# The last key tile's exponentials added by GpSimd into the last pair's sum, in a fused cross-attention and FFN kernel

## The reference, cut to what matters

```
scores = jnp.clip(jnp.einsum('bhsd,bhtd->bhst', q, k) / scale, -50.0, 50.0)
scores = jnp.where(attend, scores, -10000.0)
scores = jnp.clip(scores, -50.0, 50.0)
probs  = jax.nn.softmax(scores, axis=-1)
ctx    = jnp.einsum('bhst,bhtd->bhsd', probs, v)
```

## Time and profile before

| | |
|---|---|
| median of 3 runs | 1443.54 us (1441.85 to 1997.49) |
| the profiled execution | 1444.08 us |
| its span, first to last instruction | 1442.3 us |
| granted TensorE clock, mean | 0.998 of full speed |
| attention stage of the third entry | about 578 to 706 us in the span |
| its groups of 13 tiles | 30.95 and 30.63 us |

### The profile page before, as it was taken

How to read it: one execution, slowest core, us unless ns; L and a number is a source line. 1 busy time by engine, 2 the same in 40 slices (tenths; PEclk the granted TensorE clock), 3 DMA queues, 4 the chain that set the end, 5 groups by cost and what they waited for, 6 DMA issues and landing times. The chain is left out here.

```text
span 1442.3 us, 25135 instructions
## 1 busy us (share of the span) xinstructions
PE 1414.6 (98%) x10354; PEld 956.7 (66%) x10354; DVE 1108.7 (77%) x1659; ACT 813.2 (56%) x1021; POOL 90.1 (6%) x129
## 2 busy tenths in 40 slices
PE   9999999999999999999999999998999999999999
PEld 7886333787333688333689333486788888888887
DVE  7684999885999895899885799887865566655655
ACT  4345999435999535899635799634442333323331
POOL 1010000100000100000100000110010010100100
PEclk9999999999999999999999999999999999999999
DMA  8553000636000425000424600262345454354544
GB/s 264 143 209 152 9 10 10 190 95 240 28 10 10 147 97 189 27 17 10 141 74 173 247 12 14 59 264 103 146 147 189 167 206 167 146 190 176 207 158 175
DMA packets 54994, 180.91 MB, mean 125 GB/s; under 512 B 11249, under 2 KB 25841, under 8 KB 42721
## 3 DMA queue, kind: packets, MB, share of 16 engines
q1 hardware_dynamic: 39760, 116.08, 22.3%
q0 software_dynamic: 15120, 63.23, 12.9%
HBM read 111.97 MB, written 67.31 MB: 124 GB/s over the span
## 5 line engine op out<-in xcount | busy, mean ns | idle before, releaser
L1007 ACT ACTIVATE cx_probs<-cx_sc,proj_mbias 128x1024 f32<-128x1024 f32 (+1 forms) x416 | 442.8, 1113 | 49.9 <-PE cx_sc L1287 28.6
L1153 DVE TENSOR_SCALAR cx_probs<-cx_probs 128x1024 f32<-128x1024 f32 (+1 forms) x416 | 269.6, 683 | 52.1 <-ACT cx_probs L1007 50.1
L1119 DVE TENSOR_TENSOR cx_padd<-cx_probs,cx_probs 128x1024 f32<-128x1024 f32 x192 | 233.6, 1217 | 0.9
L1287 PEld LDWEIGHTS cx_sc<-cx_q,cx_kt 32*128 32x128 f32 (+1 forms) x2496 | 104.4, 180 | 192.8 <-ACT cx_probs L1007 173.0
L1310 PE MATMUL cx_acc<-cx_probs,cx_vt 128*32 128x512 f32 (+1 forms) x1664 | 219.0, 598 | 3.7 <-DVE cx_probs L1153 3.7
L1287 PE MATMUL cx_sc<-cx_q,cx_kt 32*128 32x512 f32 (+1 forms) x2496 | 207.7, 426 | 10.1 <-ACT cx_probs L1007 6.9
L140 PE MATMUL ff_yp<-hand_wds,ff_held 128*128 128x512 f32 x624 | 143.7, 389 | 0.1
L140 PEld LDWEIGHTS ff_yp<-hand_wds,ff_held 128*128 128x128 f32 x624 | 117.1, 188 | 24.8 <-DVE ff_kept L1832 0.5
L1769 DVE TENSOR_TENSOR ff_x<-ff_yp,ff_x 128x512 f32<-128x512 f32 x120 | 80.4, 688 | 58.4 <-PE ff_yp L140 57.7
L1322 PE MATMUL cx_tot<-cx_padd,cx_ones 128*32 128x256 f32 x1536 | 120.8, 390 | 0.0
L951 ACT ACTIVATE cx_kt<-cx_sc,proj_bk 128x256 fp32r<-128x256 f32 (+1 forms) x96 | 44.1, 478 | 70.2 <-PE cx_sc L140 69.8
(11 more groups left out here) (298 smaller groups left out, 2077.0 us busy)
## 6 DMA issues: line engine op xcount, KB each, us to landing
ff_x<-scr_x SPq DMA_DIRECT2D x30, 1024.0 KB, 5.0
scr_x<-ff_x SPq DMA_DIRECT2D x28, 1024.0 KB, 4.8
proj_raw<-in_ctxT SPq DMA_DIRECT2D x20, 512.0 KB, 6.0
hand_wds<-scr_wd POOLq DMA_DIRECT2D x7, 1024.0 KB, 10.0
scr_q<-cx_q SPq DMA_DIRECT2D x3, 2048.0 KB, 6.3
cx_wo<-scr_wo POOLq DMA_DIRECT2D x3, 2048.0 KB, 13.4
scr_xs<-cx_xs POOLq DMA_DIRECT2D x3, 2048.0 KB, 7.9
cx_q<-scr_q SPq DMA_DIRECT2D x3, 1536.0 KB, 10.5
```

The source lines that it names most:

```text
L1007: nc.scalar.activation(prob(N)[0:r], bank_of(n)[0:r], ACT.Exp, bias=mbias[0:r, b, t:t + 1], scale=SCALE).then_inc(exp_done, 1)
L1119: nc.vector.tensor_tensor(padd[z][(g * QP + j) % 2][:], prob(2 * i + z)[:], prob(2 * i + 2 + z)[:], ALU.add).then_inc(added[z], 1)
L1153: nc.vector.tensor_scalar(prob(N)[0:r], prob(N)[0:r], LOW, HIGH, ALU.max, ALU.min).then_inc(clip_done, 1)
L1287: last = nc.tensor.matmul(bank_of(2 * i + h // 2)[0:r, h % 2], kt[own, z, c, t * P:t * P + r], q[own, y, c], start=n == 0, stop=n == 2)
```

## The change

In the groups c = 0, 1 and 2 of each batch entry, `single` is no longer called. GpSimd gets a new function `last_tile`, which for z = 0 and 1 adds the 65 rows of the 13th tile's exponentials into rows 0 to 64 of the last pair sum (j = 5), in place. It waits for VectorE's add of that pair sum (`added`) and for the tile's clip (`clip_done`), and counts in a new semaphore `lent`. TensorE's `sums` of the last pair wait for both `lent`, and ScalarE's exponential that takes the 13th tile's buffer waits for `lent` in place of `single`. Group c = 3 stays as it was. The counts of `sums_done` are worked out anew, since a group now has 12 passes and only the fourth has 13. GpSimd's queue gets its six adds of an entry ahead of that entry's `beside(b)`, and those of the last entry at the end.

```
-    SUMS = 2 * QP + 1
+    PASSES = 2 * QP
...
+        def passes(g):
+            return g * PASSES + g // HC
         def sums_until(g, j):
-            return g * SUMS + 2 * j + 2 + (1 if j >= QP - 2 else 0)
+            return passes(g) + 2 * j + 2 + (1 if j >= QP - 2 and g % HC == HC - 1 else 0)
+        def lent_before(g):
+            return g - g // HC
...
+                def last_tile(b, c, z):
+                    g = b * HC + c
+                    N = (b * STEPS + (c + 1) * TT - 1) * 2 + z
+                    own = padd[z][(g * QP + QP - 1) % 2][0:TLAST]
+                    pool.wait_ge(added[z], (g + 1) * QP)
+                    pool.wait_ge(clip_done, N + 1)
+                    nc.gpsimd.tensor_tensor(own, own, prob(N)[0:TLAST], ALU.add).then_inc(lent[z], 1)
...
-                    pool.wait_ge(sums_done, (b + 1) * HC * SUMS)
+                    pool.wait_ge(sums_done, passes((b + 1) * HC))
...
-                for b in range(B - 1):
-                    beside(b)
+                for b in range(B):
+                    for c in range(HC - 1):
+                        for z in range(2):
+                            last_tile(b, c, z)
+                    if b < B - 1:
+                        beside(b)
...
-                    act.wait_ge(sums_done, (g + 1) * SUMS)
+                    act.wait_ge(sums_done, passes(g + 1))
...
+                        elif og % HC < HC - 1:
+                            act.wait_ge(lent[n % 2], lent_before(og) + 1)
                         else:
-                            act.wait_ge(sums_done, og * SUMS + SINGLE)
+                            act.wait_ge(sums_done, passes(og) + SINGLE)
...
                     for z in range(2):
+                        if j == QP - 1 and c < HC - 1:
+                            pe.wait_ge(lent[z], lent_before(g) + 1)
                         pe.wait_ge(added[z], g * QP + j + 1)
...
-                    if t == TT - 1:
+                    if t == TT - 1 and c == HC - 1:
                         single(b, c)
```

More of the change, by code:

```diff
@@ L790, in context @@
             "scores_done", "exp_done", "clip_done", "values_done", "sums_done"))
-        added = m.sems("added", 2)
+        added, lent = m.sems("added", 2), m.sems("lent", 2)
         acc_out, tot_out = m.sem("acc_out"), m.sem("tot_out")
```

## The result

The changed kernel takes 1485.89 us in the median of four runs (1484.71 to 1488.72), the kernel before 1441.85, 1443.54 and 1447.09 us beside it, with a fourth, far slower run of 1997.49 us that is left out: a ratio of 1.0285, 95% interval 1.0269 to 1.0301, so 2.7 to 3.0% slower. The profiled execution has a span of 1482.8 us where before had 1442.3, 40.5 more.

A forecast was written before the change was run, and what follows sets the result against it. TensorE, VectorE and ScalarE lay within a few per cent in attention, VectorE having 1.2 to 1.5 us free. Held, a group costs 34.05 us: 9.94 an entry, 39.8 in all, 1444.08 to 1483.9, less 0.5: 1483 us; range 1437 to 1496.

The forecast's parts named there:

- What decides is VectorE, held for the whole of each GpSimd add: Attention groups: each GpSimd add of 2.2 us stops VectorE for its whole length; chance 0.45, likeliest 1483 us.
- a transfer's issue that left the clips alone: Before the change, GpSimd issued a transfer for 1.67 us beside two clips taking 1.29 us against 1.28 elsewhere.
- The sum: VectorE's time in a lending group: 29.45 + 2 x 2.3 = 34.05 us, 39.8 us more over all batch entries.
- lost overlap: Per GpSimd add, 0.1 us more for VectorE, as two of its successive instructions no longer overlap (1.21 busy, 1.14 spacing).
- The removal's own worth: Dropping the 13th tile's product with ones gains 0.41 us a group, 4.9 us in all, if nothing else changes.
- 2.16 us loop: A tile's scores wait for the previous tile's first exponential: 0.97 scores, 1.11 exponential, 0.08 hand-offs; no step is shorter.
- The added waits are thus covered: GpSimd's adds end near 611.8 and 613.5, before their readers on ScalarE and TensorE; late only from about 4 us on.
- Rival 1: GpSimd's adds cost VectorE nothing and the removal's 4.9 us are gained: 1439 us; chance 0.27.
- Rival 2: VectorE runs at half pace while GpSimd reads: 2 x 1.2 us, 31.85 a group, +13, 1457 us; chance 0.16.
- Rival 3: GpSimd gets in only when VectorE pauses, so readers wait: 4 us a group, +48, 1491, up to 1505; chance 0.10.
- requests served in turn: Memory requests of any two engines are granted alternately; this spoke against GpSimd getting in only when VectorE pauses.
- Rival 4: TensorE idling brings 2 to 12 lower-clock stretches of 1.6 us: 3 to 19 us on top; no chance of its own.

The follow-up runs named there:

- hold-only run: Changed kernel with 24 same-size GpSimd adds on query rows no longer needed, TensorE and ScalarE not waiting for them: 1474.14 us, ratio 1.0206 to before.
- half columns: Changed kernel with GpSimd adding only 512 of 1024 elements a partition, the 13th tile left out for the others: 1458.75 us, ratio 1.0103 to before.
- memset: Changed kernel with each GpSimd add replaced by only writing ones to the 65 rows, reading nothing: 1440.31 us, ratio 0.9971 to before.
- late-signal run: Changed kernel with GpSimd setting one element instead of adding, both signals given after clips of the next group's second and third tile: 1480.69 us, ratio 1.0255.
- run without adds: Changed kernel with GpSimd's adds and their waits left out, the product with ones still gone: 1440.48 us, ratio 0.9973 to before.

## Why the prediction was right, point by point

*What decides is VectorE, held for the whole of each GpSimd add: right.* The add was put at 2.2 us between 0.9 and 2.6; it takes 2.3 alone and costs VectorE 2.19. The hold-only run shows that this suffices without any wait, the half columns that it follows the elements, the memset that it is a matter of access and not of GpSimd being busy. What the prediction had against a price, a transfer's issue that left the clips alone, doesn't hold everywhere. In the changed kernel the same issue falls so:

```profile
727.13 1.26 POOL L473 DMA_DIRECT2D cx_fl<-in_wdT  x1 [22.94 <-DMA scr_rec<-all_recip]
```

```profile
726.94 1.95 DVE L1176 TENSOR_SCALAR cx_probs<-cx_probs 128x1024 f32<-128x1024 f32 x2
```

Two clips take 1.95 us, for 1.29 elsewhere, and this makes the last lending group of the first and third entry 34.4 us and not 33.7.

*The sum: right, with its two small terms off.* It was 34.05 us a group and is 33.73. The 0.1 us for a lost overlap isn't there (2.19 is all), and VectorE's own work is 29.36, not 29.45. By groups, the stage's part was put at 39.8 us; the marks in the trace (from an entry's first clip to its last half sum, summed over the entries) give 540.5 against 503.5, 37.0. That includes some 2 us which the forecast had at nothing: two stretched clips beside an issue (1.3) and two groups with a lower clock (0.7). Nearly all of the rest of the 40.5 us is the part behind the attention, 520.4 for 516.5, which varies with a load and with the clock and isn't the change's. That the total of 1483 comes within 3 us of 1485.89 is in part luck: the stage's part was 2.8 too high, and these 3.9 weren't foreseen. The earlier trace rows carried it.

*The removal's own worth: right*, 0.41 us a group predicted, 0.38 measured over the two steps and 0.45 over all groups, by the mechanism that was given (the 2.16 us loop first, ScalarE's copy after it).

*"The added waits are thus covered": right only because the hold is worse.* The argument held the adds to be late from about 4 us on, which is so for an add that starts when asked. With GpSimd kept waiting, the signals come at 5.9 and 8.6 us, and such signals by themselves would make groups of up to 33.0 us at full clock. That a lateness of this size has a price in the order of the hold's had not been seen, in the prediction or in the expectation of the late-signal run (0 to 1 us a group, 2.4 to 2.7 measured at full clock, 32.7 to 33.0 against 30.30).

*Rivals.* Rival 1 (no price) is what the total of the memset and of the run without adds looks like, not the add. Rival 2 (half pace) is out: 2.19 of 2.3. Rival 3 described correctly that GpSimd gets in only late, after four VectorE instructions, but it needs no pause for that (ten of the twelve groups show none in front of the held clip), and the price is another: the second add follows with one clip between. The trace differs from the picture of requests served in turn, but the sum doesn't, since the same two holds are paid wherever they fall. Rival 4, the clock: the mean fell from 0.998 to 0.994. It fell in two lending groups, as the rival had it, but cost 0.3 us in each and not 1.6, since VectorE's work sets the pace there. In the late-signal run, where nothing holds VectorE, it cost 1.3 us in each of seven.

*The two rules of the Trainium skill.* The Trainium skill (SBUF — State Buffer, "Who interferes with whom") has the two engines exclude each other for whole instructions: the trace agrees, 2.19 of 2.3 us. It has VectorE's two-input instruction contend with a GpSimd instruction that reads SBUF and not with one that only writes it: the traces agree, the multiplication stretched VectorE's add from 1.21 to 2.04 us, and the memset left it alone (it stretched a clip). It also has whoever issues first get the access first, and that is not how it went: GpSimd's add at 662.64 let the clip then running and three further VectorE instructions pass, the add of 663.01 and the first two clips of the row at 664.15. The estimate of 2.2 to 2.3 us for the add from the Trainium skill (GPSIMD Engine Reference, section 3.1) was right: the trace has 2.3.

## What to carry to other kernels

An idle GpSimd is no free adder beside a VectorE that is near its limit: compare what the add would cost VectorE if it did it (1.14 us here) with what it costs to be held (2.19), and count GpSimd's time as VectorE's when its instruction reads SBUF, as the add and the multiplication did here. When several limits lie within a few per cent, taking work off one of them buys at most the distance to the next (0.38 of 0.88 us here), so the next one has to be worked out before the first is relieved. And a late signal and a held engine can cost nearly the same in total, here with the clock's help; compare groups at full clock, and move the work onto data that nobody waits for, to tell them apart.

## What the runs showed of the hardware

- GpSimd's request doesn't get in at the next boundary of VectorE's back-to-back instructions. The first add's recorded 5.02 us are 2.8 of waiting and 2.2 of work. It enters before the second tile's first clip in all twelve groups, also when it asks 2.4 us later. That this clip is the first whose exponential is only just ready (a gap of 0.21 and 0.24 us stands before it in two groups of the changed kernel, and 0.20 to 0.31 us in three of the run that asks later) may be the reason; it wasn't tried.
- A GpSimd multiplication of one tensor by a constant isn't cheaper than the add of two: two of them take 8.57 us beside VectorE, for 7.79 to 7.82, and they stretch adds as well as clips, in smaller pieces.
- An add of a tensor with itself, rounded to the matmul's format, held VectorE for 1.71 us against 2.19. Whether that is the single source or the 64 rows for 65 isn't parted.
- GpSimd's issue of a transfer can hold VectorE too: one of 1.26 us stretched a clip from 0.69 to 1.34 us, while one of 1.67 us in the kernel before stretched none.
- An accumulating transfer of 260 KB within SBUF took 5.9 us to land.
